# Turning the attention's input on VectorE instead of TensorE, and cutting the keys at 128, in a three-part decoder block

## What is computed

```
x1 = layernorm(x  + fourier_mix(x))          # 8 heads of 64; fft of q, k, v, running sum over tokens, inverse fft, w_out
q, k, v = x1 @ W_q + b_q, ctx @ W_k + b_k, ctx @ W_v + b_v      # ctx: 77 keys an image; 16 heads of 32
p  = softmax(where(mask == 0, -1e6, q k^T / sqrt(32)))
x2 = layernorm(x1 + (p v) @ W_o + b_o)
y  = layernorm(x2 + x2 @ W + bias)           # W: an int4-quantized kernel with a rank-16 part merged into it
```

## Time and profile before

| what | us |
|---|---|
| median of 3 runs | 945.8 (941.78 to 947.99) |
| the profiled execution, own time | 944.69 |
| its span, first to last instruction | 942.9 |

### The profile page before, as it was taken

How to read it: one execution, slowest core, us unless ns; L and a number is a source line. 1 busy time by engine, 2 the same in 40 slices (tenths; PEclk the granted TensorE clock), 3 DMA queues, 4 the chain that set the end, 5 groups by cost and what they waited for, 6 DMA issues and landing times.

```text
span 942.9 us, 14474 instructions
## 1 busy us (share of the span) xinstructions
PE 892.1 (95%) x4348; PEld 739.6 (78%) x4348; DVE 674.7 (72%) x1132; ACT 377.3 (40%) x1403; POOL 376.6 (40%) x338
## 2 busy tenths in 40 slices
PE   5798999999999999999689999999999999999997
PEld 4683888888888888888568788888888888888775
DVE  3364566666665757667578878889788897888957
ACT  4161221202121111001596466665656656566611
POOL 2000464435354343333236534335343453434723
PEclk9897999999999999999799999999999999999999
DMA  6961811331404020204503040321303214031021
GB/s 183 284 201 57 173 39 53 82 91 44 134 11 122 22 67 23 67 38 140 175 16 109 21 135 15 93 71 26 133 13 91 71 28 131 13 91 23 14 78 46
DMA packets 85211, 76.03 MB, mean 81 GB/s; under 512 B 39143, under 2 KB 57831, under 8 KB 85167
## 3 DMA queue, kind: packets, MB, share of 16 engines
q1 hardware_dynamic: 85167, 75.49, 27.1%
HBM read 52.60 MB, written 22.87 MB: 80 GB/s over the span
## 4 chain that ended last, share of the span: by engine, by line
PE 42%; DVE 4%; ACT 2%; issue 2%; POOL 2%; POOLq 0%; DVEq 0%
PE shared_ps L114 31%; PE score_ps L114 4%; PE shared_ps L1185 4%; ACT probs L1391 1%; PE shared_ps L1148 1%; PE shared_ps L1218 1%; POOL probs L1540 1%; DVE score_ps L1697 1%; DVE xT_lo L1654 1%; DVE x_and_res L1743 0%; DVE pT_lo L1681 0%; DVE top_s L1702 0%; POOL x_and_res L1555 0%; DVE y L1721 0%; DVE w_o_lo L1864 0%
## 5 line engine op out<-in xcount | busy, mean ns | idle before, releaser
L1391 ACT ACTIVATE probs<-score_ps,top_s 128x77 f32<-128x77 f32 x512 | 159.1, 359 | 36.8 <-DVE top_s L1702 36.8
L1391 ACT ACTIVATION_READ_ACCUMULATOR probs<-score_ps,top_s 128x1 f32 x512 | 122.9, 240 | 0.0
L1540 POOL TENSOR_TENSOR probs<-probs,per_total 128x616 f32<-128x616 f32 x64 | 82.7, 1309 | 64.7 <-DVE per_total L1709 64.5
L1533 POOL TENSOR_TENSOR rstd<-ve,half_power 128x1 f32<-128x1 f32 x64 | 42.4, 662 | 156.7 <-DVE ve L1732 152.2
L1697 DVE COPY_PREDICATED score_ps<-hidden,masked 128x616 f32<-128x616 int32 x64 | 67.2, 1050 | 9.4 <-PE score_ps L114 9.3
L97 POOL TENSOR_TENSOR xT_lo<-x_tok,xT_hi 128x512 fp32r<-128x512 f32 x28 | 39.0, 1394 | 85.6 <-ACT xT_hi L93 85.6
L1398 ACT ACTIVATE pT_hi<-shared_ps 103x512 fp32r<-103x512 f32 (+1 forms) x96 | 54.9, 614 | 45.1 <-PE shared_ps L1185 44.6
L713 ACT ACTIVATE qT_hi<-vals 128x512 fp32r<-128x512 f32 x32 | 19.3, 628 | 119.2 <-POOL vals L760 103.9
L760 POOL TENSOR_TENSOR vals<-qs_prod 128x512 f32<-128x512 f32 x32 | 41.0, 1293 | 62.7 <-DVE qs_prod L846 62.7
L1681 DVE TENSOR_TENSOR pT_lo<-shared_ps,pT_hi 103x512 fp32r<-103x512 f32 (+1 forms) x96 | 64.5, 684 | 0.0
L706 ACT ACTIVATE v_sb<-v_ps 128x512 f32<-128x512 f32 x32 | 18.9, 594 | 106.9 <-PE v_ps L114 106.9
(11 more groups left out here) (210 smaller groups left out, 2642.5 us busy)
## 6 DMA issues: line engine op xcount, KB each, us to landing
x_tok<-in_x SPq DMA_DIRECT2D x32, 256.0 KB, 4.6
x_res<-in_x SPq DMA_DIRECT2D x8, 1024.0 KB, 7.3
x_between<-mix_x SPq DMA_DIRECT2D x32, 256.0 KB, 2.0
x<-x_between SPq DMA_DIRECT2D x8, 1024.0 KB, 5.6
x_tok<-x_between SPq DMA_DIRECT2D x8, 1024.0 KB, 5.7
out<-y_out SPq DMA_DIRECT2D x32, 256.0 KB, 2.0
wqkv_sb<-in_w_qkv SPq DMA_DIRECT2D x16, 192.0 KB, 5.0
keys_split<-w_q_hi SPq DMA_DIRECT2D x8, 154.0 KB, 5.0
```

What stands on the lines that cost most here:

```text
L1391: nc.scalar.activation(probs[:, t % 2, j * KEYS:(j + 1) * KEYS], score_ps[:, g, k * KEYS:(k + 1) * KEYS], ACT.Exp, bias=top[:, t % 2, j:j ...
L1533: nc.gpsimd.tensor_tensor(rstd[:, n:n + 1], ve[:, n:n + 1], half_power[:], ALU.pow).then_inc(rstd_ready, 1)
L1540: nc.gpsimd.tensor_tensor(p, p, per_total[:, t % 2, h * heads:(h + 1) * heads].unsqueeze(2) .to_broadcast([P, heads, KEYS]), ALU.mult).the ...
```

## The change

- `turn_x1` leaves TensorE. x1 is loaded in quarters (four DMAs in place of one), VectorE transposes it in place, one column of blocks at a time (four instructions an image), ScalarE makes the high part from SBUF, and GpSimd makes the low part (`low_of_column`) in place of VectorE. The uses X0 to X3 are gone from the order of the banks. Both ScalarE and GpSimd now wait themselves until O3 is made.
- The first Q of an image waits for all four high and all four low parts.
- In the hand-over at the end of `mix_tokens` the same is done for image 0, with the low part on VectorE.
- W_q is loaded with its rows in matching order, by 16 DMAs in place of one.
- Keys are cut at 128 across a pair of groups (616 keys-by-heads: four chunks of 128 and a tail of 104), so a block of tokens takes 10 transposes in place of 12; P{t}0 and P{t}1 hold four chunks each, P{t}2 the two tails. P{t}0 now waits only for the first half of the normalized probabilities. The number of matmuls in `weigh_values` stays. The values are loaded by 24 DMAs an image in place of 12.

```diff
+def group_chunks(g):
+    h, first = g // 2, 2 * (g % 2)
+    return [(m, chunk_at(h, first + m), TAIL if first + m == 4 else CHUNK) for m in range(3)]
```

The hand-over, on TensorE between the two halves of the last products, and on VectorE after its last step:

```diff
-                if half == 0:
-                    pe.wait_ge(x1_loaded, 16)
-                    pe.wait_ge(kv_done, nth(B - 1, 8, 7))
-                    pe.wait_ge(qs_done, nth(B - 1, 8, 7))
-                    for c in range(NC):
-                        for t in range(NT):
-                            last = nc.tensor.transpose(next_banks[c][:, t * P:(t + 1) * P],
-                                                       x1_next[:, t, c * P:(c + 1) * P], ident[:])
-                        last.then_inc(hand.filled, 1)
...
+            dve.wait_ge(x1_loaded, 16 * NC)
+            for c in range(NC):
+                turn_block_column(nc, x1_next, c, hand.x1_turned)
             for c in range(NC):
                 dve.wait_ge(hand.x1T_hi, c + 1)
-                nc.vector.tensor_tensor(x1T[1][:, c, :], next_banks[c][:], x1T[0][:, c, :].bitcast(F32),
-                                        ALU.subtract).then_inc(hand.freed, 1)
+                low_of_column(nc.vector, x1T, x1_next, c, hand.x1T_lo)
```

The order of the banks, and what SyncE and TensorE do:

```diff
 BANK_ORDER = ["V0", "V1", "V2", "V3", "O0", "P00", "O1", "P01", "O2", "T0", "P02", "F0", "P10", "P11", "T1",
-              "O3", "X0", "X1", "X2", "F1", "X3", "T2", "P12", "Q0", "F2", "P20", "P21", "Q1", "T3", "Q2",
+              "O3", "F1", "T2", "P12", "Q0", "F2", "P20", "P21", "Q1", "T3", "Q2",
               "P22", "F3", "P30", "P31", "P32", "Q3"]
...
             def load_x1(i):
                 wait_reuse(sp, x1T_hi, i * NC)
-                sp.dma_start(x1[:], x1_dram[i].rearrange("(t p) d -> p t d", p=P)).then_inc(x1_loaded, 16)
+                wait_reuse(sp, x1T_lo, i * NC)
+                load_quarters(sp, x1, x1_dram[i], x1_loaded)
...
             def project_q(i, s, c):
                 use = f"Q{c}"
                 if c == 0:
                     pe.wait_ge(x1T_hi, nth(i, NC, NC - 1))
-                    pe.wait_ge(freed, s.emptied("X3"))
+                    pe.wait_ge(x1T_lo, nth(i, NC, NC - 1))
...
             def turn_probs(i, s, t, c):
-                if c == 0:
-                    pe.wait_ge(normed, nth(i, NT * 2, 2 * t + 1))
+                if c < 2:
+                    pe.wait_ge(normed, nth(i, NT * 2, 2 * t + c))
...
                 score(i, s, 2, 1)
-                turn_x1(i + 1, s, 0)
-                turn_x1(i + 1, s, 1)
-                turn_x1(i + 1, s, 2)
                 project_f(i, s, 1)
-                turn_x1(i + 1, s, 3)
                 turn_x2(i, s, 2)
```

On ScalarE, and then on GpSimd with its place in GpSimd's `step`:

```diff
             def split_x1(i, s, c):
-                use = f"X{c}"
-                act.wait_ge(filled, s.filled(use))
-                nc.scalar.activation(x1T[0][:, c, :], shared_ps[s.bank(use)][:], ACT.Copy).then_inc(x1T_hi, 1)
+                act.wait_ge(x1_turned, nth(i, NC, c))
+                if c == 0:
+                    after_projection(act, i, s)
+                high_of_column(nc, x1T, x1, c, x1T_hi)
...
+            def split_x1(i, s, c):
+                pool.wait_ge(x1T_hi, nth(i, NC, c))
+                if c == 0:
+                    after_projection(pool, i, s)
+                low_of_column(nc.gpsimd, x1T, x1, c, x1T_lo)
...
                 bias_x2(i, s, 3)
                 normalize_probs(i, 2, 0)
+                split_x1(i + 1, s, 0)
                 root(i, s, "F1")
                 normalize_probs(i, 2, 1)
+                split_x1(i + 1, s, 1)
+                split_x1(i + 1, s, 2)
+                split_x1(i + 1, s, 3)
                 root(i, s, "F2")
```

In VectorE's `step`:

```diff
                 split_probs(i, s, 0, 0)
+                turn_x1(i + 1, 0)
                 add_o(i, s, 1)
...
                 split_probs(i, s, 0, 1)
+                turn_x1(i + 1, 1)
                 invert_totals(i, 1)
                 add_o(i, s, 2)
                 normalize_o(i, s, 1)
                 split_x2(i, s, 0)
                 measure(i, s, "O2")
+                turn_x1(i + 1, 2)
                 split_probs(i, s, 0, 2)
+                turn_x1(i + 1, 3)
...
                 softmax_top(i, 2, 1)
-                split_x1(i + 1, s, 0)
                 measure(i, s, "O3")
-                split_x1(i + 1, s, 1)
-                split_x1(i + 1, s, 2)
                 normalize_o(i, s, 3)
                 add_f(i, s, 1)
                 invert_totals(i, 2)
-                split_x1(i + 1, s, 3)
```

More of the change, by code:

```diff
@@ L36 @@
 GK = GH * KEYS
-KC = [(0, 103), (103, 103), (206, 102)]
+HALF = 2 * GK
+CHUNK = 128
+TAIL = HALF - 4 * CHUNK
+BANKS = [(0, 4, CHUNK), (4, 4, CHUNK), (8, 2, TAIL)]
 RANK = 16
@@ L85, in load_interleaved, with load_quarters @@
         sp.dma_start(tile[q * BLOCK:(q + 1) * BLOCK, j, :], w[at:at + BLOCK, :]).then_inc(loaded, 16)
+def load_quarters(sp, tile, src, loaded):
+    for q, part in enumerate(by_quarter(src)):
+        sp.dma_start(quarters(tile)[q * BLOCK:(q + 1) * BLOCK, :, :], part).then_inc(loaded, 16)
 def turn_block_column(nc, tile, j, turned):
@@ L228, in _ @@
             sp.wait_ge(ctx_turned, NC)
-            for q, src in enumerate(by_quarter(ins["x"][0])):
-                sp.dma_start(quarters(x_first)[q * BLOCK:(q + 1) * BLOCK, :, :], src).then_inc(hand.x_loaded, 16)
+            load_quarters(sp, x_first, ins["x"][0], hand.x_loaded)
             sp.wait_ge(w_turned, 3)
@@ L566, in load_x @@
                     sp.wait_ge(x_lo, nth(i - 2, NC, NC - 1))
-                for q, src in enumerate(by_quarter(x[i])):
-                    sp.dma_start(quarters(x_tok[half])[q * BLOCK:(q + 1) * BLOCK, :, :], src).then_inc(x_loaded[half], 16)
+                load_quarters(sp, x_tok[half], x[i], x_loaded[half])
             def load_residual(i):
@@ L676, in _ @@
                         last.then_inc(out_filled, 1)
[L677 to L686 removed]
+            pe.wait_ge(kv_done, nth(B - 1, 8, 7))
+            pe.wait_ge(qs_done, nth(B - 1, 8, 7))
             pe.wait_ge(hand.x1T_hi, NC)
[L689 removed]
+            pe.wait_ge(hand.x1T_lo, NC)
             for c in range(NC):
@@ L731, in _ @@
             for c in range(NC):
+                act.wait_ge(hand.x1_turned, c + 1)
+                high_of_column(nc, x1T, x1_next, c, hand.x1T_hi)
+            for c in range(NC):
                 act.wait_ge(hand.filled, c + 1)
-                nc.scalar.activation(x1T[0][:, c, :], next_banks[c][:], ACT.Copy).then_inc(hand.x1T_hi, 1)
-            for c in range(NC):
-                act.wait_ge(hand.filled, NC + c + 1)
                 nc.scalar.activation(qT[0][:, c, :], next_banks[c][:], ACT.Identity,
@@ L1052, in norm_count, with after_projection @@
             return nth(i - 1, 2 * NT, s.norms.index(use))
+        def after_projection(eng, i, s):
+            if "O3" in s.order:
+                eng.wait_ge(filled, s.filled("O3"))
         def x2T_of(i, t):
@@ L1141, in _ @@
         def _(pe):
-            def turn_x1(i, s, c):
-                if c == 0:
-                    pe.wait_ge(x1_loaded, nth(i, 1, 0) * 16)
-                use = f"X{c}"
-                wait_reuse(pe, freed, s.reusable(use))
-                for t in range(NT):
-                    last = nc.tensor.transpose(shared_ps[s.bank(use)][:, t * P:(t + 1) * P],
-                                               x1[:, t, c * P:(c + 1) * P], ident[:])
-                last.then_inc(filled, 1)
             def project_q(i, s, c):
@@ L1590, in _ @@
             normalize_probs(0, 1, 1)
+            for c in range(NC):
+                split_x1(1, Shared(0, False, True, True), c)
             normalize_probs(0, 2, 0)
@@ L1835, in _ @@
             softmax_top(0, 2, 1)
+            for c in range(NC):
+                turn_x1(1, c)
             split_probs(0, s, 0, 0)
```

95 lines of the change are left out of this document (47 added, 48 removed).

## The result

The changed kernel takes 1018.07 us (median of 4 runs, 1016.27 to 1020.37), the kernel before 946.89 (4 runs beside it): a ratio of 1.0754, 95% interval 1.0727 to 1.0781. The profiled execution took 1019.65, its span is 1017.9, so 75.0 us more than the span before.

What follows compares the result with a forecast made beforehand. Prediction: TensorE and VectorE balance a step's first half, then TensorE alone sets the pace. Per step 8.3 + 1.8 = 10.1; six steps 60.6, start +2.2, hand-over -0.4: +62.4 on 944.7 gives 1007 us; own bounds 1000 to 1014, range 988 to 1022.

Steps and rivals of the forecast that it cites:

- the last rival: Low parts and turns both dear, by SBUF contention or waits at F0 and O3: 12.5 a step, 1021 us; chance 0.11.
- GpSimd's chain: Before Q0: four low parts at 1.30 us behind GpSimd's normalizations and root F1; Q0 8.9 us later a step.
- The clock: Behind TensorE's pause before Q0: half clock for some 3.7 us of work, costing 1.8 us a step, bounds 0 to 5.
- From Q0 to `bias_x2(3)`: Rest of a step: VectorE's turns less removed work, +0.40 before `add_f(1)`; TensorE's tails -0.44; VectorE's shrinking waits a little less.
- F0's wait: TensorE's 0.50 us wait before F0: two turns stand ahead of its input; upper bound 2.5 for VectorE's delay, 0.4 taken.
- Start stage: Before the first Q0: low parts end near 483.4, so +1.5, or +2.2 with a chance of half clock; bounds 0 and 4.
- After the last Q0: Closing stage: waits on GpSimd and VectorE in turn; 8 fewer transposes bring at most 0.9 us, counted 0.
- Hand-over: End of `mix_tokens`: second half of the products could begin at 436.20, when GpSimd's last remainder ends, not 436.67; -0.4 us.
- Loads: SyncE's extra DMA issues for x1 and values: cost nothing; without the room up to 12 us a step.
- The clock stays up: Rival: TensorE's clock does not fall through the pauses before Q0; 996 us; chance 0.14.
- VectorE hiding the pause: Rival: VectorE becomes the bound and the pause before Q0 hides behind it; 945 us; chance 0.03.
- The faster rival: TensorE stays the bound, GpSimd's fourth low part arrives before Q0; saves 2.6 us a step, 927 us; chance 0.04.

Runs made afterwards that it cites:

- lows_twice: The changed kernel with GpSimd making each low part of a step twice; 1054.82 us, ratio 1.1149 to the kernel before.
- lows_early: The changed kernel with GpSimd's low parts earlier in its order and ScalarE's fourth high part ahead of exponentials(2,1); 964.17 us, ratio 1.0180 to the kernel before.
- pause_filled: The changed kernel with 36 extra matmuls of 512 columns in TensorE's wait before Q0; 1010.46 us, ratio 1.0675 to the kernel before.
- turns_late: The changed kernel with VectorE's turns 0 and 1 of x1 moved later, next to turns 2 and 3; 1019.73 us, ratio 1.0778 to the kernel before.
- ahead_start: ahead_shared with earlier highs and moved turns in the start stage, plus 28 extra identity transposes on TensorE; 940.84 us, ratio 0.9953 to the kernel before.
- keys_in_128: The kernel before with only its keys cut in chunks of 128, x1 still transposed by TensorE; 940.70 us, ratio 0.9935 to the kernel before.
- turns_first_lows_early: As lows_early, with VectorE's four turns of x1 moved to the beginning of the step; 955.75 us, ratio 1.0096 to the kernel before.
- ahead_shared: The changed kernel with x1 of image i+2 loaded and turned in step i, low parts split between GpSimd and VectorE; 945.05 us, ratio 0.9989 to the kernel before.

## Why the prediction was right, and where it was off

The direction, the place and the mechanism came as predicted, and 1018 lies in the range, but 11 us above the forecast and 4 above the forecast's own bounds. It is inside the range only by the bound that the last rival set, and what that rival asked of the low parts did not happen; so far the number was lucky. The steps of the forecast:

- **GpSimd's chain.** From `bias_x2(3)` to Q0: 9.95 after, 1.09 before, so +8.9; forecast 8.5 (8.9 less VectorE's 0.4). The lows took 1.81 + 3.85 = 5.66 for 5.19, the first one beside VectorE's masking. lows_twice shows the chain on the path, lows_early that its place in the order is what counts.
- **The clock**, forecast 1.8 a step. pause_filled shows 2.3. This is one mis-sized term, 0.5 in each of six steps. In one of the last five steps it includes a fall that the prediction didn't have, in the middle of F0 (0.67 in 665.07 to 669.17).
- **From Q0 to `bias_x2(3)`.** In the step of pause_filled that has the clock at 1.00 (68.42, with 9.9 from `bias_x2(3)` to Q0) this takes 58.5; before it was 58.70 less 1.09, 57.6. So VectorE's and TensorE's balance is +0.9 where I had -0.2 (0.40, less 0.44 for the tails and 0.15). Most of the difference is VectorE's stretch from the masking to `add_f(1)`, 26.25 in that step for 25.14, so +1.1 where I had 0.40:

```profile
654.45 1.68 DVE L1719 COPY_PREDICATED score_ps<-hidden,masked 128x616 f32<-128x616 int32 x1
...
680.70 0.68 DVE L1743 TENSOR_TENSOR y<-shared_ps,x_and_res 128x512 f32<-128x512 f32 x1
```

The sum had put the wait for GpSimd's root of O3 at nothing. In the changed kernel it is 0.76, because the low parts that left VectorE had stood there; they saved less than their 1.81. That this is the whole of the 0.7 was not tried by itself. F0's wait (1.95 for 0.50), which I had kept only as an upper bound, is TensorE's side of the same stretch: turns_late took it down to 0.78, and the stretch stayed.

- **Start stage**, forecast +2.2 with the chance of half clock. Q0 came 2.05 later and then ran 5.3 us instead of 2.75. In the kernel before the granted clock was 1.00 from 475 to 485, with TensorE's transposes of x1 in that stretch. That their loss lets the clock fall is not shown: ahead_start, which put others in their place, did not settle it, and in keys_in_128, which keeps them, the clock fell just ahead of Q0 (485.42) all the same (columns as in the earlier trace rows):

```profile
478.90:482.40 3.50, 3.50 (x18) 3.47 (x17) 2.30 (x5) 3.01 (x17) 0.00 (x0) 0.51 0.09 15
```

- **After the last Q0**, forecast 0: 115.6 us for 111.05. Of it 3.1 went with the clock in pause_filled, which has 112.5 there; nearly all of the other 1.4 stands in keys_in_128 too (112.4). So the cut at 128 makes the closing stage longer, where I had counted no change: two uses of F wait 1.57 and 1.70 us there for VectorE (875.69 and 890.94 in keys_in_128), where up to the last F the longest wait of the kernel before was 0.80.
- **Added up.** Five steps at +12.1 (8.9, 2.3 and 0.9) and a first one at +7.6 make 68.4 against the forecast's 60.6, the start 2.05 against 2.2, the end 4.6 against 0, together 75.0 against 62.4. Why the first step grew by less was not tried.
- **Hand-over** -0.4: image 0's first masking came 0.2 later, too small to follow. The second half of the products waited for GpSimd's remainder, as I had put it, but began no sooner than in the earlier trace rows:

```profile
436.87 0.50 PE L694 MATMUL out_ps<-w_back_hi,qT_hi 128*128 128x512 f32 x1 [1.11 <-POOL qT_lo L779]
```

- **Loads** at nothing. x1's four issues took 1.95 on SyncE where one took 0.41, ahead of values of 1.0 an issue as before:

```profile
712.47 1.95 SPq L93 DMA_DIRECT2D x<-x_between  x4
...
722.37 4.01 SPq L1118 DMA_DIRECT2D v_block_hi<-values_split  x4
```

They are wanted from 729 on and no turn of a step waited for one; turns_first_lows_early shows that this room is gone once the turns move forward.

Of the rivals, the one with dear low parts gives almost the measured number, 1021, but not for its reasons: the lows cost 0.5 a step more, not 2. Its other part, 0.5 a step for waits at F0 and O3, points at the stretch in which the forecast missed 0.7. "The clock stays up" is excluded by the rows at 0.50, and VectorE hiding the pause by the wait of 9.31. The faster rival named its own condition, the last low before TensorE reaches Q0; lows_early comes within 0.9 us of it and is still slower than before, and ahead_shared, as near, gives back 0.8 us a step. No kernel met the condition in full, but these two say that the rival priced it too high: it valued a step's 2.6 us of transposes in full, though VectorE paces the half most of them lie in, as the prediction itself had said elsewhere.

## What to carry to other kernels

Work moved to an idle engine costs first by its place in that engine's list (the same lows took 1018 us at the end of it and 964 earlier): read what the engine is doing, and waiting for, at the moment when the result is wanted. Where two engines pace a stage together, taking work from one of them and putting part on the other is worth little there (0.8 of 2.5 us a step at best here); take the saving that needs no one else first (here the cut at 128). A pause put before a long product costs twice, once as itself (9.3 us here) and once in TensorE's clock behind it (2.3).
